# Performer layer: key maximum by a transposition on PE, norms behind the exponents, bfc ahead of Wo; experts: gate inside the first W1 product

## The chip, the cores and the metric

One core of a Trainium2 chip runs the whole kernel in one launch. The metric is the device time in microseconds; three runs of the kernel before gave 673.88, 672.17 and 673.33, median 673.33.

## The reference, cut to what matters

Three residual layers act on x (256 rows of 256 numbers): a cross attention over 4096 context rows, a Performer attention, and a mixture of experts. The last two matter here, each behind a layer norm.

```python
# Performer: 16 heads of 16 numbers, proj 44 x 16
td   = einsum('bhnd,md->bhnm', t * dn, proj)           # the exponents
diag = 0.5 * dn**2 * sum(t * t, axis=-1)               # the squared norms
mx   = max(td, -1) if is_query else max(td, (-1, -2))  # keys: one maximum per head over all rows
feat = ratio * (exp(td - diag - mx) + 1e-4)
k_sum = sum(kp, -2); d_inv = 1 / einsum('bhnm,bhm->bhn', qp, k_sum)
out  = einsum('bhmd,bhnm,bhn->bhnd', einsum('bhnm,bhnd->bhmd', kp, v), qp, d_inv)
y    = relu((out @ Wo.T + bo) @ Wfc.T + bfc)
# experts: 8 and a shared one, all computed for all 256 rows, F = 1024
probs = softmax(x @ Wg); the two largest are normalised to the weights cw
out   = sum_e cw[e] * (silu(x @ W1[e] + b1[e]) @ W2[e] + b2[e]) + 0.1 * shared(x)
```

## The kernel before, in words

Each engine has its own instruction queue, and the order in it is written out by hand; queues meet only through counting semaphores. PE is TensorE, DVE VectorE, ACT ScalarE, POOL GpSimd, SP issues transfers. `attention`, `performer` and `experts` each are one block, and all engines meet between blocks. Products that need precision split each operand into a rounded high part and a low part (what the rounding left) and sum three products (`part_products`, L165 to L170). `keep_busy` (L173 to L177), called `busy` in the Performer, is a dummy product on PE whose result nobody reads; each call is two instructions in the trace, as every matmul in float32 is.

**Performer** (L980 to L1304). Everything lives in one PSUM tile `ps` of eight banks; keys use banks 0 to 3, queries 4 to 7, each for two row tiles j times two halves of the heads. PE transposes the normalised rows, computes keys and queries transposed (L1075), and then, per tile and half, the exponents (L1085) and into the eight columns beside them the norms (L1087). DVE takes maxima of the key tiles (L1251), joins them (L1253) and takes the maxima of the query tiles (L1257). The key maximum over the 128 rows is an all-reduce over partitions on POOL (L1064). PE goes on with the values (L1111). DVE adds norm and maximum (`less`, L1260 and L1272) and subtracts it from the exponents (`shift`, L1244), first queries, then, behind the values' bias (L1267), keys; ACT takes the exponentials (L1196). PE transposes the query features (L1122), adds the constant feature's part with two products over `v_one` (L1130) and the key features' products (L1135). From that come denominators (L1145) and numerators (L1152); DVE inverts and multiplies per half (L1291, L1294), PE multiplies by Wo (L1160), ACT adds bo (`h_t`, L1206), PE puts bfc into banks 0 and 1 (L1167) and adds the products with Wfc (L1172), and DVE adds the rectified result to `x_res` (L1302). Between these steps PE has `busy` calls. On the side DVE makes the low part of the second expert's W1 (L1298).

**Experts** (L1307 to L1629). After the norm PE transposes z (L1412). DVE copies it to `zt` (L1577, L1580) for the gate, ACT makes the high part `zp` (L1520, L1522), DVE the low part (L1583). PE computes the gate (L1419), then W1 of experts 0 and 1 (`up`, L169), then W2 of 0 (`down`, L1447), and from there `up` of the next and `down` of the last in turns. `h_ps` has four banks of two tiles. DVE takes the gate's logits through some twenty small operations, each waiting for the one before, to `share` (L1587 to L1607), and only behind these makes W2's low part (`lo2`, L1547) and splits the activations in two halves (`split_act`: a cast L1556, a subtraction L1558 each). ACT makes the gate's exponentials, the silus (L1510), then the high parts of W2 of the next expert (L1500) and of W1 of the one behind that (L1494), which releases POOL's low part of that W1 (L1393).

## Time and profile before

| | us |
|---|---|
| median of three runs | 673.33 |
| profiled execution, its own time | 672.22 |
| its span, first to last instruction | 670.5 |
| PE busy | 651.6 (97%) |
| DVE busy | 511.7 (76%) |
| ACT busy | 414.2 (62%) |
| POOL busy | 271.8 (41%) |

The cross attention ends at about 522.7 us of the span, the Performer at 557.4, the experts at the end. All times in the rows below are microseconds from the start of the span. In a timeline a row is a run of like instructions: start, duration of the whole, engine, line, operation, output and inputs with their shapes, count, and in brackets how long the engine had been idle and for whom. PEld is the loading of weights into PE, which overlaps with its products.

### The profile page before, as it was taken

The numbers are of one execution on the slowest core, as the hardware profiler recorded it, in microseconds if no ns is written. First come the engines' busy times: TensorE is split into PE (matmuls) and PEld (weight loads), VectorE is DVE, ScalarE is ACT, GpSimd is POOL, SyncE is SP. The second block draws the span as 40 slices with busy tenths as digits, with TensorE's granted clock in tenths as the row PEclk, the third lists the DMA queues.
The fourth block names the chain that finished last, engine by engine and source line by source line (L and its number), as shares of the span: only waits on it lengthen the run. The fifth ranks groups of instructions, "written<-read, shape, count | busy, mean of one in ns | idle before, by whom it ended". The sixth has DMA issues, their size and how long they took to land. (4 is left out here: it accounts for less than half of the span.)

```text
span 670.5 us, 14507 instructions
## 1 busy us (share of the span) xinstructions
PE 651.6 (97%) x5192; PEld 522.4 (78%) x5192; DVE 511.7 (76%) x1008; ACT 414.2 (62%) x880; POOL 271.8 (41%) x211
## 2 busy tenths in 40 slices
PE   8899999999999999999999999999999999899998
PEld 7677777777777777777777777777775778899998
DVE  4888898877878777778767867877777685987674
ACT  5788788866566666665667566556563433655651
POOL 3544545533443443433443434434431300364640
PEclk9999999999999999999999999999999999999999
DMA  7111340010000010000000000000000301566500
GB/s 213 56 44 33 112 162 1 17 33 1 1 17 1 2 49 1 1 1 1 17 1 1 2 0 2 1 17 2 1 1 1 127 1 65 189 212 218 163 33 17
DMA packets 26164, 30.51 MB, mean 46 GB/s; under 512 B 4201, under 2 KB 23794, under 8 KB 26098
## 3 DMA queue, kind: packets, MB, share of 16 engines
q1 hardware_dynamic: 24594, 28.86, 13.1%
q8 instruction: 39, 0.64, 0.4%
q10 hardware_dynamic: 1504, 0.79, 0.4%
q14 instruction: 27, 0.22, 0.1%
HBM read 29.38 MB, written 0.26 MB: 44 GB/s over the span
## 5 line engine op out<-in xcount | busy, mean ns | idle before, releaser
L897 POOL TENSOR_TENSOR k_rms<-k_ss,neg_half 128x4 f32<-128x4 f32 x136 | 189.2, 1391 | 242.7 <-DVE k_ss L771 242.7
L603 ACT ACTIVATE probs<-s_ps,minus_bound 128x512 f32<-128x512 f32 x272 | 164.7, 689 | 97.0 <-PE s_ps L436 97.0
L169 PE MATMUL kv_ps<-w_quad,xn 128*128 128x512 f32 x816 | 206.9, 402 | 5.2 <-DVE xn L718 3.9
L765 DVE SCALAR_TENSOR_TENSOR probs_sum<-probs,tile_mask,probs_sum 128x512 f32<-128x512 f32 x264 | 191.8, 744 | 4.9 <-ACT probs L603 4.8
L169 PEld LDWEIGHTS kv_ps<-w_quad,xn 128*128 128x128 f32 x816 | 147.8, 188 | 44.5 <-DVE xn L718 6.6
L449 PE MATMUL o_ps<-probs,v 128*64 128x256 f32 x1088 | 132.6, 385 | 0.8 <-ACT probs L603 0.7
L436 PEld LDWEIGHTS s_ps<-q_parts,kt 64*128 64x128 f32 x1632 | 101.2, 185 | 26.6 <-issue 20.0
L436 PE MATMUL s_ps<-q_parts,kt 64*128 64x256 f32 x1632 | 115.0, 287 | 0.3 <-DVE kt L775 0.2
L449 PEld LDWEIGHTS o_ps<-probs,v 128*64 128x64 f32 x1088 | 71.9, 136 | 42.0 <-issue 10.9
L749 DVE SCALAR_TENSOR_TENSOR kn<-k_rms,kv_ps 128x256 f32<-128x256 f32 x136 | 56.8, 417 | 53.0 <-POOL k_rms L897 51.8
L771 DVE TENSOR_REDUCE k_ss<-k_sq 128x4 f32<-128x256 f32 x136 | 56.4, 415 | 21.0 <-ACT k_sq L581 20.0
L595 ACT ACTIVATE kt<-s_ps 128x256 fp32r<-128x256 f32 x136 | 44.8, 380 | 42.1 <-PE s_ps L420 42.1
L588 ACT ACTIVATE v<-kv_ps,tile_mask 128x256 f32<-128x256 f32 x136 | 66.9, 492 | 0.0
L775 DVE TENSOR_TENSOR kt<-s_ps,kt 128x256 fp32r<-128x256 f32 x136 | 51.4, 419 | 17.6 <-ACT kt L595 17.3
L581 ACT ACTIVATE k_sq<-kv_ps 128x256 f32<-128x256 f32 x136 | 53.9, 396 | 1.3 <-PE kv_ps L169 1.3
L420 PE MATMUL s_ps<-ident,kn 128*128 128x128 f32 x272 | 41.2, 273 | 0.7 <-DVE kn L749 0.5
L420 PEld LDWEIGHTS s_ps<-ident,kn 128*128 128x128 f32 x272 | 33.7, 140 | 10.0 <-DVE kn L749 0.9
L1393 POOL TENSOR_TENSOR w_first<-w_raw,w_first 128x2048 fp32r<-128x2048 f32 x4 | 21.8, 5462 | 29.2 <-ACT w_first L1494 29.2
L1556 DVE CAST e_act_p<-e_act_f 128x1024 fp32r<-128x1024 f32 x18 | 17.9, 994 | 20.4 <-PE e_y_ps L1447 20.3
L1510 ACT ACTIVATE e_act_f<-e_h_ps,e_b_now 128x256 f32<-128x256 f32 x72 | 27.9, 481 | 7.1 <-DVE e_act_p L1558 4.6
L169 PE MATMUL e_h_ps<-e_zp,w_first 128*128 128x256 f32 x240 | 28.6, 278 | 0.0
L169 PEld LDWEIGHTS e_h_ps<-e_zp,w_first 128*128 128x128 f32 x240 | 28.0, 188 | 0.3 <-issue 0.3
(212 smaller groups left out, 647.3 us busy)
## 6 DMA issues: line engine op xcount, KB each, us to landing
w_raw<-in_ffn_W SPq DMA_DIRECT2D x18, 1024.0 KB, 5.6
rows<-in_ctx SPq DMA_DIRECT2D x7, 512.0 KB, 4.0
w_raw<-in_L_xattn_Wkv SPq DMA_DIRECT2D x6, 256.0 KB, 3.4
wout<-in_L_xattn_Wout SPq DMA_DIRECT2D x4, 256.0 KB, 2.8
wq_raw<-in_L_xattn_Wq SPq DMA_DIRECT2D x3, 256.0 KB, 2.8
rows<-in_ctx SPq DMA_DIRECT2D x2, 256.0 KB, 5.3
w_raw<-in_L_xattn_Wkv ACTq DMA_DIRECT2D x2, 256.0 KB, 5.2
wq_raw<-in_L_xattn_Wq ACTq DMA_DIRECT2D x1, 256.0 KB, 4.3
```

What stands on the lines that cost most here:

```text
L169: last = nc.tensor.matmul(out, stationary(k, s), moving(k, m), start=n == 0, stop=n == len(terms) - 1)
L420: last = nc.tensor.transpose(kt_ps(n)[:, j * P:(j + 1) * P], kn[n % 2][:, j].rearrange("p c d -> p (c d)"), ident[:])
L436: last = nc.tensor.matmul(s_ps[b][c][:, j, :], kt[b][half, s, j * P:(j + 1) * P], q_parts[g % 2][half, j, m, :], start=term == 0, stop=ter ...
L449: last = nc.tensor.matmul(o_ps[g % 2][c * DH:(c + 1) * DH, j, :], v[n % V_RING][:, j, c, :], probs[n % P_RING][:, j, c, :], start=t == 0 a ...
L581: nc.scalar.activation(k_sq[n % 2][:].rearrange("p j c d -> p (j c d)"), kv_ps[n % 2][:, 0, :], ACT.Square, scale=DH ** -0.5).then_inc(sq_ ...
L588: nc.scalar.activation(v[n % V_RING][:].rearrange("p j c d -> p (j c d)"), kv_ps[n % 2][:, 1, :], ACT.Copy, scale=tile_mask[:, t:t + 1]).t ...
L603: nc.scalar.activation(probs[n % P_RING][:, :, c, :], s_ps[n % 2][c][:], ACT.Exp, bias=minus_bound[:]).then_inc(exp_done, 1)
L749: nc.vector.scalar_tensor_tensor(kn[n % 2][:], k_rms[n % 2][:].unsqueeze(3).to_broadcast([P, 2, 2, DH]), 1.0 / RMS_FLOOR, kv_ps[n % 2][:, ...
L765: nc.vector.scalar_tensor_tensor(total, probs[n % P_RING][:, :, c, :], seen, total, ALU.mult, ALU.add).then_inc(sum_done, 1)
L771: nc.vector.reduce_sum(k_ss[n % 2][:], k_sq[n % 2][:], AX_X).then_inc(ss_done, 1)
L775: nc.vector.tensor_tensor(kt[n % 2][:, 1, :], kt_ps(n), kt[n % 2][:, 0, :].bitcast(F32), ALU.subtract).then_inc(kt_lo, 1)
L897: nc.gpsimd.tensor_tensor(k_rms[n % 2][:].rearrange("p i c -> p (i c)"), k_ss[n % 2][:].rearrange("p i c -> p (i c)"), neg_half[:, 0:4], A ...
```

## The change

In the Performer the norm products leave the exponent groups. All exponents come first; the key maximum, now taken on each row, is transposed by PE (`top_turned`), reduced by DVE to one number per head, set on a 16x16 diagonal, and spread over all rows by a product with ones (`top_spread`). This product and the norms of queries and keys come behind the last exponents, into free columns of banks 0 to 3. POOL's all-reduce is gone. DVE makes the `less` of queries and keys directly after each other; the values on PE wait for it. The keys' first shift stands before the values' bias, the second behind it and behind a new sum `v_sum` of the two value tiles, with which the constant feature needs one product. The bfc products go in front of Wo, in banks 0 and 7, in place of dummies; other dummies are dropped.

In the experts the high part of `zp` is made as each half is transposed, the low part from PSUM, and the copies `zt` for the gate behind these. `up` of expert 0 starts without the gate; the gate's products come in it behind its first bank.

```diff
-        top_key = sb("top_key", [P, 2, H])
+        top_key, top_all, top_diag = sb("top_key", [P, H]), sb("top_all", [H, 1]), sb("top_diag", [H, H])
+        top_spread, v_sum = sb("top_spread", [P, H]), sb("v_sum", [P, H * VW])
...
-        def diagonal(n):
-            b = bank(n, 0, 0)
-            return ps[:, b:b + 4, EW:EW + HH]
+
+        def norm_ps(n):
+            at = 488 if n == QUERY else EW
+            return ps[:, 0:4, at:at + HH]
+
+        top_turned_ps, top_spread_ps = ps[0:H, 0, 360:360 + P], ps[:, 0, 496:496 + H]
+
+        def fc_ps(j):
+            return ps[:, 7 if j else 0, 0:D]
...
                                     ALU.subtract).then_inc(ew.w1_lo, 1)
-            pool.wait_ge(key_top, 1)
-            nc.gpsimd.partition_all_reduce(top_key[:, 1, :], top_key[:, 0, :], P, bass.bass_isa.ReduceOp.max).then_inc(key_top_all, 1)
             nc.gpsimd.iota(ew.number[:], [[1, E]], base=0, channel_multiplier=0).then_inc(ew.numbered, 1)
...
-            def exponents_of(n, parts_done, done):
+            def exponents_of(n, j, parts_done, done):
+                for half in range(KD):
+                    if j == 0:
+                        pe.wait_ge(parts_done, half + 1)
+                    last = part_products(nc, ps[:, bank(n, j, half), 0:EW], lambda k, s: qk_t[:, n, half, s, j * P:(j + 1) * P],
+                                         lambda k, s: proj_p[:, s, :], 1)
+                last.then_inc(done, 1)
+
+            def norms_of(n):
                 for j in range(QT):
                     for half in range(KD):
-                        if j == 0:
-                            pe.wait_ge(parts_done, half + 1)
-                        b = ps[:, bank(n, j, half)]
-                        part_products(nc, b[:, 0:EW], lambda k, s: qk_t[:, n, half, s, j * P:(j + 1) * P],
-                                      lambda k, s: proj_p[:, s, :], 1)
-                        last = nc.tensor.matmul(b[:, EW:EW + HH], qk_sq[:, n, half, j * P:(j + 1) * P],
-                                                diag_bd[:], start=True, stop=True)
-                    last.then_inc(done, 1)
+                        last = nc.tensor.matmul(norm_ps(n)[:, 2 * j + half, :], qk_sq[:, n, half, j * P:(j + 1) * P], diag_bd[:],
+                                                start=True, stop=True, skip_group_check=True)
+                return last
...
             pe.wait_ge(fw.blocks_done, 2)
-            exponents_of(KEY, k_lo, k_exponents)
-            pe.wait_ge(q_lo, KD)
-            exponents_of(QUERY, q_lo, q_exponents)
+            for j in range(QT):
+                exponents_of(KEY, j, k_lo, k_exponents)
+            exponents_of(QUERY, 0, q_lo, q_exponents)
             pe.wait_ge(key_top, 1)
+            nc.tensor.transpose(top_turned_ps, top_key[:], ident[:]).then_inc(top_turned, 1)
+            exponents_of(QUERY, 1, q_lo, q_exponents)
+            pe.wait_ge(top_placed, 1)
+            norms_of(QUERY)
+            norms_of(KEY)
+            nc.tensor.matmul(top_spread_ps, ones[0:H, :], top_diag[:], start=True, stop=True, skip_group_check=True).then_inc(diagonals_done, 1)
...
             pe.wait_ge(k_shifted, 2)
             pe.wait_ge(v_kept, 1)
-            for j in range(QT):
-                nc.tensor.matmul(ps[0:PAIR, 0, 0:NPAIR * 2 * VW], feat_eps[:], v_one[:, j].rearrange("p h d -> p (h d)"),
-                                 start=j == 0, stop=False, skip_group_check=True)
+            nc.tensor.matmul(ps[0:PAIR, 0, 0:NPAIR * 2 * VW], feat_eps[:], v_sum[:], start=True, stop=False, skip_group_check=True)
...
                 last.then_inc(o_done, 1)
-            busy(7, 3)
+            for j in range(QT):
+                nc.tensor.matmul(fc_ps(j), ones[0:1, :], spread["bfc"][0:1, :], start=True, stop=False)
...
                 if k == 0:
-                    busy(7, 3)
-            for j in range(QT):
-                nc.tensor.matmul(ps[:, j, 0:D], ones[0:1, :], spread["bfc"][0:1, :], start=True, stop=False)
-            busy(7, 1)
+                    busy(3, 2)
             for k in range(KD):
                 pe.wait_ge(ht_kept, k + 1)
                 for j in range(QT):
-                    last = nc.tensor.matmul(ps[:, j, 0:D], h_t[:, k, j * P:(j + 1) * P], w["Wfc"][:, k, :],
+                    last = nc.tensor.matmul(fc_ps(j), h_t[:, k, j * P:(j + 1) * P], w["Wfc"][:, k, :],
...
-            busy(7, 3)
+            busy(3, 1)
...
-            nc.vector.tensor_tensor(top_key[:, 0, :], top[:, KEY, 0:KD].rearrange("p k h -> p (k h)"),
+            nc.vector.tensor_tensor(top_key[:], top[:, KEY, 0:KD].rearrange("p k h -> p (k h)"),
...
-            for j in range(QT):
-                dve.wait_ge(q_exponents, j + 1)
-                last = nc.vector.reduce_max(top[:, QUERY, 2 * j:2 * j + 2], exponents(QUERY, j), AX_X)
-            last.then_inc(own, 1)
+            dve.wait_ge(q_exponents, 1)
+            nc.vector.reduce_max(top[:, QUERY, 0:2], exponents(QUERY, 0), AX_X)
+
+            dve.wait_ge(top_turned, 1)
+            nc.vector.reduce_max(top_all[:], top_turned_ps, AX_X).then_inc(top_found, 1)
+            dve.wait_ge(top_found, 1)
+            nc.vector.tensor_scalar(top_diag[:], ident[0:H, 0:H], top_all[:], None, ALU.mult).then_inc(top_placed, 1)
+            dve.wait_ge(q_exponents, 2)
+            nc.vector.reduce_max(top[:, QUERY, 2:4], exponents(QUERY, 1), AX_X).then_inc(own, 1)
             dve.wait_ge(own, 3)
-            nc.vector.tensor_tensor(less[:, QUERY], diagonal(QUERY), top[:, QUERY], ALU.add).then_inc(q_less, 1)
+            dve.wait_ge(diagonals_done, 1)
+            nc.vector.tensor_copy(top_spread[:], top_spread_ps).then_inc(spread_kept, 1)
+            nc.vector.tensor_tensor(less[:, QUERY], norm_ps(QUERY), top[:, QUERY], ALU.add).then_inc(q_less, 1)
+            dve.wait_ge(spread_kept, 1)
+            nc.vector.tensor_tensor(less[:, KEY].rearrange("p (j k) h -> p j (k h)", j=QT).rearrange("p j (k h) -> p j k h", k=KD),
+                                    norm_ps(KEY).rearrange("p (j k) h -> p j k h", j=QT),
+                                    top_spread[:].rearrange("p (k h) -> p k h", k=KD).unsqueeze(1).to_broadcast([P, QT, KD, HH]),
+                                    ALU.add).then_inc(k_less, 1)
             dve.wait_ge(q_less, 1)
             for j in range(QT):
                 shift(QUERY, j, q_shifted)
+            dve.wait_ge(k_less, 1)
             dve.wait_ge(v_done, 1)
+            shift(KEY, 0, k_shifted)
...
-            last.then_inc(v_kept, 1)
-            dve.wait_ge(key_top_all, 1)
-            nc.vector.tensor_tensor(less[:, KEY].rearrange("p (j k) h -> p j (k h)", j=QT).rearrange("p j (k h) -> p j k h", k=KD),
-                                    diagonal(KEY).rearrange("p (j k) h -> p j k h", j=QT),
-                                    top_key[:, 1, :].rearrange("p (k h) -> p k h", k=KD).unsqueeze(1).to_broadcast([P, QT, KD, HH]),
-                                    ALU.add).then_inc(k_less, 1)
-            dve.wait_ge(k_less, 1)
-            for j in range(QT):
-                shift(KEY, j, k_shifted)
+            last.then_inc(v_biased, 1)
+            dve.wait_ge(v_biased, 1)
+            nc.vector.tensor_tensor(v_sum[:], v_one[:, 0].rearrange("p h d -> p (h d)"), v_one[:, 1].rearrange("p h d -> p (h d)"),
+                                    ALU.add).then_inc(v_kept, 1)
+            shift(KEY, 1, k_shifted)
...
-                last = nc.vector.scalar_tensor_tensor(x_res[:, j, :], ps[:, j, 0:D], 0.0, x_res[:, j, :], ALU.max, ALU.add)
+                last = nc.vector.scalar_tensor_tensor(x_res[:, j, :], fc_ps(j), 0.0, x_res[:, j, :], ALU.max, ALU.add)
...
-            keep_busy(nc, h_ps[:, 0, :], ident[:], x_res[:, 0, :], 2)
-            pe.wait_ge(zt_kept, KD)
-            pe.wait_ge(wg_in, 16)
-            for j in range(QT):
-                for k in range(KD):
-                    last = nc.tensor.matmul(gate_ps[:, j * E:(j + 1) * E], zt[:, k, j * P:(j + 1) * P], wg[:, k, :],
-                                            start=k == 0, stop=k == KD - 1)
-            last.then_inc(logits_done, 1)
-            pe.wait_ge(zp_done, 1)
-
-            def up(t):
+            pe.wait_ge(zp_done, KD)
+
+            def gates():
+                pe.wait_ge(zt_kept, KD)
+                pe.wait_ge(wg_in, 16)
+                for j in range(QT):
+                    for k in range(KD):
+                        last = nc.tensor.matmul(gate_ps[:, j * E:(j + 1) * E], zt[:, k, j * P:(j + 1) * P], wg[:, k, :],
+                                                start=k == 0, stop=k == KD - 1)
+                last.then_inc(logits_done, 1)
+
...
                     last.then_inc(up_done, 1)
+                    if gated and b == 0:
+                        gates()
...
-            up(Turn(0, 2))
+            up(Turn(0, 2), gated=True)
...
-            act.wait_ge(zt_done, KD)
-            nc.scalar.activation(zp[:, 1, 0, :], y_ps[1][:, 0, :], ACT.Copy).then_inc(zp_hi, 1)
-            act.wait_ge(zt_kept, 1)
-            nc.scalar.activation(zp[:, 0, 0, :], y_ps[0][:, 0, :], ACT.Copy).then_inc(zp_hi, 1)
+            for k in range(KD):
+                act.wait_ge(zt_done, k + 1)
+                nc.scalar.activation(zp[:, k, 0, :], y_ps[k][:, 0, :], ACT.Copy).then_inc(zp_hi, 1)
...
-            dve.wait_ge(zt_done, 1)
-            nc.vector.tensor_copy(zt[:, 0, :], y_ps[0][:, 0, :]).then_inc(zt_kept, 1)
-            dve.wait_ge(zt_done, KD)
-            dve.wait_ge(zp_hi, 1)
-            nc.vector.tensor_copy(zt[:, 1, :], y_ps[1][:, 0, :]).then_inc(zt_kept, 1)
-            dve.wait_ge(zp_hi, KD)
-            dve.wait_ge(zt_kept, KD)
-            nc.vector.tensor_tensor(zp[:, :, 1, :], zt[:], zp[:, :, 0, :].bitcast(F32), ALU.subtract).then_inc(zp_done, 1)
+            for k in range(KD):
+                dve.wait_ge(zp_hi, k + 1)
+                nc.vector.tensor_tensor(zp[:, k, 1, :], y_ps[k][:, 0, :], zp[:, k, 0, :].bitcast(F32), ALU.subtract).then_inc(zp_done, 1)
+            for k in range(KD):
+                nc.vector.tensor_copy(zt[:, k, :], y_ps[k][:, 0, :]).then_inc(zt_kept, 1)
```

## Rows read from the trace of the kernel before

**Rows 1.** The page: busy time of the engines, and the chain that ended last.

```profile
PE 651.6 (97%) x5192; PEld 522.4 (78%) x5192; DVE 511.7 (76%) x1008; ACT 414.2 (62%) x880; POOL 271.8 (41%) x211
...
PE e_y_ps L1447 6%; PE e_h_ps L169 6%; DVE e_act_p L1558 1%; PE e_h_ps L177 0%; PE e_y_ps L1462 0%; PE e_bias_ps L1462 0%; DVE w_first L1547 0%; DVE e_act_p L1556 0%; DVE e_picked L1605 0%; PE e_gate_ps L1419 0%; PE e_bias_ps L1482 0%; ACT 
```

**Rows 2.** Windows: span, busy us (instructions) of PE, PEld, DVE, ACT, POOL; clock, DMA.

```profile
536.40:541.90 5.50, 4.92 (x39) 4.27 (x37) 5.20 (x10) 2.32 (x3) 0.39 (x1) 1.00 0.00 0
...
574.80:583.90 9.10, 7.21 (x55) 6.46 (x53) 9.07 (x5) 2.90 (x7) 5.01 (x2) 1.00 0.52 189
...
583.90:668.00 84.10, 83.92 (x721) 83.72 (x720) 60.77 (x57) 44.36 (x69) 38.07 (x12) 1.00 0.41 137
```

**Rows 3.** Timeline of the Performer's key maximum: start, us, engine, line, operation.

```profile
532.36 0.89 DVE L1251 TENSOR_REDUCE f_top<-f_ps 128x16 f32<-128x704 f32 x1
...
534.70 0.17 DVE L1253 TENSOR_TENSOR f_top_key<-f_top 128x16 f32<-128x16 f32 x1
...
536.39 1.87 PEld L1111 LDWEIGHTS f_ps<-f_Wv,f_zt 128*128 128x128 f32 x16
...
537.75 1.69 DVE L1244 TENSOR_TENSOR f_feats<-f_ps,f_less 128x704 f32<-128x704 f32 x2
...
538.00 0.39 POOL L1064 PARTITION_ALL_REDUCE f_top_key<-f_top_key  x1 [5.59 <-issue]
...
539.35 0.75 DVE L1267 TENSOR_TENSOR f_v_one<-f_ps,f_bv 128x256 f32<-128x256 f32 x2
```

**Rows 4.** Timeline, PE's weight loads of eps and context products.

```profile
541.98 0.69 PEld L1130 LDWEIGHTS f_ps<-f_v_one,f_feat_eps 128*88 128x88 f32 x4 [0.66 <-DVE f_feats L1244]
...
542.74 2.74 PEld L1135 LDWEIGHTS f_ps<-f_v_one,f_feats 128*88 128x88 f32 x32
```

**Rows 5.** Timeline, from the second Wo group to the next block.

```profile
551.47 0.84 PEld L1160 LDWEIGHTS f_ps<-f_o_t,f_Wo 128*128 128x128 f32 x4
...
552.31 0.91 ACT L1206 ACTIVATE f_h_t<-f_ps,f_bo 128x256 f32<-128x256 f32 x2 [7.77 <-PE f_ps L1160]
...
552.64 0.72 PEld L1167 LDWEIGHTS f_ps<-f_bfc,ones 1*128 1x128 f32 x4 [0.33 <-issue]
...
554.01 1.70 PEld L1172 LDWEIGHTS f_ps<-f_Wfc,f_h_t 128*128 128x128 f32 x8
...
555.73 0.86 DVE L1302 SCALAR_TENSOR_TENSOR x_res<-f_ps,x_res 128x256 f32<-128x256 f32 x2 [2.23 <-PE f_ps L1172]
...
555.96 1.46 PE L177 MATMUL f_ps<-f_Wq,ident 128*128 128x256 f32 x6
...
557.71 0.75 DVE L965 BATCH_NORM_STATS2 e_stats<-x_res 128x6 f32<-128x256 f32 x2 [1.13 <-PEq L987]
```

**Rows 6.** Timeline of the experts' start: high part, gate, first W1 product, share.

```profile
561.45 0.38 ACT L1520 ACTIVATE e_zp<-e_y_ps 128x256 fp32r<-128x256 f32 x1 [8.23 <-PE e_y_ps L1412]
...
562.41 0.97 PEld L1419 LDWEIGHTS e_gate_ps<-e_wg,e_zt 128*128 128x128 f32 x8 [0.54 <-DVE e_zt L1580]
...
563.29 5.72 PEld L169 LDWEIGHTS e_h_ps<-e_zp,w_first 128*128 128x128 f32 x48
...
563.50 0.39 DVE L1587 MAX8 e_logit_top<-e_gate_ps 128x8 f32<-128x8 f32 x2 [0.35 <-PE e_gate_ps L1419]
...
565.06 1.28 ACT L1510 ACT_TABLE_LOAD   x1 [0.33 <-PE e_h_ps L169]
...
569.48 2.29 DVE L1547 TENSOR_TENSOR w_first<-w_raw,w_first 128x2048 fp32r<-128x2048 f32 x1
```

**Rows 7.** Timelines of POOL, DVE and PE where the first expert is split.

```profile
573.80 4.88 POOL L1393 TENSOR_TENSOR w_first<-w_raw,w_first 128x2048 fp32r<-128x2048 f32 x1 [13.73 <-ACT w_first L1494]
...
574.27 5.50 DVE L1558 TENSOR_TENSOR e_act_p<-e_act_f,e_act_p 128x1024 fp32r<-128x1024 f32 x1
...
579.82 3.10 PE L1447 MATMUL e_y_ps<-w_first,e_act_p 128*128 128x256 f32 x24 [1.89 <-DVE e_act_p L1558]
...
603.79 1.74 DVE L1556 CAST e_act_p<-e_act_f 128x1024 fp32r<-128x1024 f32 x1 [3.27 <-PE e_y_ps L1447]
```

More of the change, by code:

```diff
@@ L1017, in performer @@
         k_exponents, q_exponents = sem("f_k_exponents"), sem("f_q_exponents")
-        key_tops, key_top, key_top_all = sem("f_key_tops"), sem("f_key_top"), sem("f_key_top_all")
+        key_tops, key_top, top_turned = sem("f_key_tops"), sem("f_key_top"), sem("f_top_turned")
+        top_found, top_placed, diagonals_done = sem("f_top_found"), sem("f_top_placed"), sem("f_diagonals_done")
+        v_biased, spread_kept = sem("f_v_biased"), sem("f_spread_kept")
         k_less, q_less, k_shifted, q_shifted = sem("f_k_less"), sem("f_q_less"), sem("f_k_shifted"), sem("f_q_shifted")
```

2 lines of the change are left out of this document (added).

## The prediction

> **What bounds the kernel now.** I read the busy shares of the page first, then the chain that ended last, then the windows by stage, and only then the timeline of each engine. PE is busy for 97% of the span, and the part of the chain that the page shows starts at 557.7 us and is nearly all PE work of the experts [rows 1]. From 583.9 us PE does not idle until the end [rows 2]: whatever is won or lost before that point moves the end by the same amount, and nothing behind it is changed. Ahead of it are two places where PE does not set the pace. In the Performer, PE is filled with dummy products (L177), so its busy share hides the real chain, which runs PE, DVE and ACT in turn; I follow it from the first exponents (530.6) to the residual add (L1302). In the first two experts PE idles 1.9 us in the stretch from 574.8 to 583.9 [rows 2]. The reader is to see there that the second half of L1558 takes 5.50 us, where the other halves take 1.23, and lies just behind the start of the POOL subtraction L1393 [rows 7].
>
> Sums are made on the profiled execution: span 670.5, its own time 672.22, so 1.72 lies around the span. The median shown, 673.33, is 1.11 above it. I add the sum to the median.
>
> **Performer, key maximum and norms.** Until 530.6 nothing changes. Before, each of the eight exponent groups on PE ended with a norm product; now the groups follow without them, and DVE's first maximum still starts at 532.36, since the low part of the queries (L1240) leaves DVE only then. One maximum over 704 columns takes 0.89 and back to back they come every 0.80 to 0.85 [rows 3], so the second ends at 534.04 and the key top is there at 534.25, where it stood at 534.87 (534.70 + 0.17) [rows 3]: 0.6 earlier. Then a new chain: the transposition on PE (no row of this shape; a matmul that begins alone took 0.28 to 0.29 to its end, and 0.06 to be released) ends at 534.62, while DVE is in its maximum of the first query tile (534.20 to 535.09). The maximum over 16x128 and the small product behind it are new shapes. From below two 0.17 instructions bound them, by the 128x16 row of [rows 3], from above two of 0.89. I take 0.29 and 0.24, by the 128-column and the 128x8 operations elsewhere in the trace, as they are nearest in size. PE gets its release at 535.63, just as its second query group has been issued.
>
> Now eight norm products and the spread product, two weight loads each, 18 in all. The loads of L1111 come every 0.117 (16 in 1.87) [rows 3], those of the gate every 0.12 (8 in 0.97) [rows 6]; a product that sits between others costs at most its full load, 0.19. Bounds 1.9 to 3.4, I take 2.05 by the nearest rows, and 0.2 for the last one's drain: 537.88. DVE copies the spread and makes both sums (0.37 to 0.6, by the 0.17 to 0.19 of such small operations): the first query shift starts at 538.25, where it was 537.75 [rows 3], 0.5 later. The value products L1111, which used to lie under the query maxima, now wait for the key sums: 538.35 plus 2.05 is 540.4, before 538.45. DVE ends the query shifts at 539.94 and idles 0.46, since the first key shift is queued behind the wait for the values. Then 0.89 (key shift 0), 0.66 for the two value adds as they pipeline (0.75 with the end of the second [rows 3]), 0.44 for the new 128x272 sum (bounds 0.29 for 128 columns, 0.69 for 512), 0.89 (key shift 1): 543.29, before 541.92 (540.23 + 1.69 for two such shifts). That is +1.37. The PE transposes of the queries, behind the later values, end at 543.05 and stay just covered. The eps product is one call in place of two: of the 0.76 between the first load of L1130 and that of L1135 [rows 4] half goes, -0.37. The exponentials of the keys are there in time (544.1 for the second tile, PE needs it at 545.1). Term: **+1.0**, bounds 0.0 (the shift chain no later than PE's own work) to +2.9 (all new shapes at their upper ends).
>
> What goes for this is the all-reduce on POOL [rows 3]. DVE did not wait for it: behind L1267 (539.35 + 0.75) it goes on at 540.02 without idling. Its removal by itself is worth nothing; it was hidden behind the query side.
>
> **Performer, bfc and Wo.** Up to L1160 everything follows the DVE reciprocals, so the bfc products in place of three dummies stay covered (0.72 of loads against 1.16; cover gone would cost at most 0.7). The second Wo group waited for its dummies (551.47 against its input at 551.29): -0.12. Then the real gain: ACT has h_t ready at 552.31 + 0.47 = 552.78 and the other half at 553.22, but PE first loads bfc (552.64) and a dummy and starts Wfc only at 554.01 [rows 5]. With these gone Wfc starts 0.06 behind h_t, at 552.72 after the 0.12: **-1.29**, and its second k finds its input (553.1) before it needs it (553.6). What is late next is L1298 on DVE, which ends at 553.49, earlier than the Wfc result (554.44), so it does not bind.
>
> **Performer, end.** The residual add ends at 555.73 + 0.86 = 556.59, but the six dummy instructions on PE end at 555.96 + 1.46 = 557.42, and DVE starts the next block at 557.71 [rows 5]. At the change of block before this one DVE was last (522.68) and started 0.32 later (523.00). With two dummy instructions PE ends 0.9 sooner and DVE binds: 555.30 + 0.32 = 555.62 against 557.71 is -2.09 with the last term in it, so **-0.80** of its own (bounds 0 and -0.83). Start of the experts: +1.0 - 1.29 - 0.80 = about -1.1.
>
> **Experts, on PE.** Times here are in the old frame. The high parts on ACT follow each transposed half: 561.23 to 561.61, then 561.51 to 561.89 (0.38 each, 0.28 apart); the low parts on DVE (0.42 each) end at 562.46, and W1 starts at 562.52, where the gate products started at 562.41 [rows 6]. The gate cost the same 0.88 before its successor could load, in front of W1 or inside it. So PE ends both W1 products 0.1 later than before and gains nothing: the two copies that DVE now makes later had not been the limit, as the gate only went first.
>
> **Experts, on DVE and ACT.** The gate now comes behind twelve products (12 x 0.118 = 1.42, from 48 loads in 5.66 [rows 6]): the logits come at 565.03 instead of 563.50, 1.53 later. The small operations from the logits to the share, 6.06 us, have to run ahead of L1547, which starts then at 571.0 [rows 6]; the first half of L1556 follows at 573.21 and that of L1558 at 573.93 to 575.16. On ACT the table load no longer waits for W1 (565.06 was the end of the first bank [rows 6]); it comes behind the exponentials at 566.25, the eight silus (3.02 to 3.08) end at 570.6, two 1.92 copies follow 1.8 apart, and POOL is released at 574.27 instead of 573.80. PE needs the first half of the split at 574.95; it comes at 575.2, 0.2 late.
>
> The price lies in the second half. [Rows 7] show POOL released at 573.80, in the middle of a DVE cast (to 574.23), POOL ending at 578.68, and the L1558 that followed the cast held until then: POOL had waited for one DVE operation and then had its way for 4.45 us before the next. The cast of 603.79 is held in the same way (1.74 for 0.69). So I let POOL, released at 574.27, wait for the end of the first half of L1558 (575.16) and hold its successors to 579.61. Then the cast needs 0.55 more and L1558 1.25: PE gets the second half at 581.5, before 579.82. **+1.69**, and its idle time there grows from 1.9 to some 3. Everything behind it shifts as it is, PE bound.
>
> The Trainium skill ("SBUF — State Buffer", section "SBUF: two separate sides") says that DVE and GpSimd share a port pair as an exclusive lock for a whole instruction, DVE casts in a fast mode and operations with two SBUF inputs included, the loser fully blocked. The rows agree, and by that rule the term stays +1.69; it says nothing of who goes next when DVE's queue is full, on which rival 1 hangs.
>
> **Sum.** +1.0 - 1.29 - 0.80 + 1.69 = +0.6: 672.22 + 0.6 = 672.8 for an execution like the profiled one, 673.33 + 0.6 = **673.9** for the median. No difference that can be told: a measurement of this kernel tells about 0.3%, 2 us, from nothing.
>
> **Rivals.**
> 1. POOL never gets between. If the operations in DVE's queue keep POOL out until the second L1558 has begun (575.9), PE has its input at 577.1 and does not idle: -1.1 - 1.9 = -3.0, 670.3. For it: POOL comes later relative to PE. Against: it would have to be 1.6 later than I work out, and at 573.80 it won against a full DVE queue. 0.14.
> 2. POOL comes in 0.37 or more sooner relative to DVE, inside the first cast (to 573.90). Then both halves of L1558 lie behind it: the first half at 579.4, the second at 581.3, while PE does both after 579.5 and ends at 585.6 instead of 582.9: +2.7 - 1.1 = +1.6, 674.9. For it: the margin is small. Against: ACT's chain is made of measured pieces. 0.15.
> 3. The granted clock falls. It is 1.00 in every stage, also where PE idles 0.6 and is busy 4.92 of 5.5 [rows 2]. Now PE has two us of eight-column products, a pause of half a us and sparser value products in a row (535.6 to 540.4), and fewer dummies later. At 1.2 GHz in place of 2.4 that stretch's 4.9 us of work could take up to that much more; as half of it is loads and waits I take +3 on top of the sum: +3.6, 677. The point from which it decides is the norm products. No row shows the lower level, and PE's idling of 1.9 us at 577.9 did not bring it. 0.12. The Trainium skill ("TensorE: Matmul & The Clock Gate", "Part 1: The HAM clock gate") has the clock set by how busy PE was of late, between just these two levels; by it the thinned stages are what could bring the fall, no run yet shows it.
> 4. The gain at the end of the Performer does not come, because the change of block takes its time from something else than PE's dummies: +0.6 + 0.8 = +1.4, 674.7. 0.07.
>
> **How the numbers follow.** The forecast has the remaining 0.52, with its own range 672.6 to 675.2 (the terms' likely errors, 0.7, and the spread of medians). Faster than 671.3 is nearly only rival 1: 0.15. Slower than 675.3 is rival 3, and the upper part of rival 2, rival 4 and of the first term's bounds: 0.24. Range 670.7 to 676.4: it leaves out half of rival 1 and most of rival 3.
>
> **What would show it.** Right: the first query shift 0.3 to 0.8 later, L1244's last of the keys about 1.4 later and context about 1.0; Wfc directly behind h_t; experts starting 0.8 to 1.4 earlier; the logits 1.5 later against the block's start; the second L1556 or L1558 of the first expert held behind POOL and PE idle some 3 us there. Wrong: a clock below 1.00; the second L1558 at 1.23 us; an exponent or norm stage more than 1 us off.

## The result

| | before | changed |
|---|---|---|
| median of six runs each, same chip | 672.08 us | 676.13 us |
| ratio, 95% interval | | 1.0049 [1.0037, 1.0060] |
| profiled execution, its own time (span) | 672.22 (670.5) | 675.89 (674.2) |
| mean granted clock of the profiled execution | 1.000 | 0.992 |

The change costs 4 us where I had forecast +0.6. The time itself lies in the range (to 676.4), near rival 3, the fall of the clock, which I had given 0.12. That it lies in the range is partly luck: I had counted from 673.33, the median of three runs, and the median of six is 672.08. Counted from there the same range ends at 675.2, below the measured time.

First the windows of the changed kernel, with the columns of [rows 2] (the fraction before the last two figures is the granted clock):

```profile
536.00:538.00 2.00, 1.47 (x13) 1.35 (x12) 0.55 (x5) 0.00 (x0) 0.00 (x0) 1.00 0.00 0
...
538.00:540.00 2.00, 1.97 (x12) 1.97 (x13) 1.57 (x2) 1.18 (x2) 0.00 (x0) 0.72 0.00 0
...
540.00:542.00 2.00, 2.00 (x9) 1.82 (x8) 0.82 (x2) 0.40 (x1) 0.00 (x0) 0.50 0.00 0
...
542.00:544.00 2.00, 2.00 (x17) 1.81 (x17) 1.97 (x5) 0.79 (x1) 0.00 (x0) 0.92 0.00 0
...
574.00:580.00 6.00, 3.80 (x31) 3.31 (x29) 5.97 (x3) 1.57 (x4) 5.71 (x2) 0.99 0.95 346
...
580.00:590.00 10.00, 9.03 (x48) 8.41 (x49) 8.63 (x11) 5.01 (x6) 0.00 (x0) 0.67 0.55 189
...
590.00:674.00 84.00, 81.49 (x702) 81.29 (x700) 54.03 (x52) 41.77 (x68) 38.17 (x12) 1.00 0.35 119
```

Two stretches stand out: from 538.9 to 542.3 and from 579.9 to 586.7 the clock is at 1.2 GHz instead of 2.4 (0.50 of full speed where a window lies inside). Before, the clock was 1.00 in every window [rows 2]. Ahead of the first, PE works on the norms (536 to 538: busy 1.47 of 2) and pauses; ahead of the second it idles 2.2 us in the window from 574 to 580 and one more after it.

The timeline of DVE and of PE's weight loads, which answers to [rows 3]. The whole block starts 0.32 us earlier than before, which belongs to the attention; I count it out below.

```profile
532.01 1.68 DVE L1264 TENSOR_REDUCE f_top<-f_ps 128x16 f32<-128x704 f32 x2
...
537.90 1.68 DVE L1257 TENSOR_TENSOR f_feats<-f_ps,f_less 128x704 f32<-128x704 f32 x2
...
541.18 0.89 DVE L1257 TENSOR_TENSOR f_feats<-f_ps,f_less 128x704 f32<-128x704 f32 x1 [1.60 <-PE f_ps L1128]
...
543.12 0.88 DVE L1257 TENSOR_TENSOR f_feats<-f_ps,f_less 128x704 f32<-128x704 f32 x1
```

```profile
535.20 1.86 PEld L1097 LDWEIGHTS f_ps<-f_diag_bd,f_qk_sq 128*128 128x128 f32 x16 [0.29 <-DVE f_top_diag L1274]
...
538.03 2.74 PEld L1128 LDWEIGHTS f_ps<-f_Wv,f_zt 128*128 128x128 f32 x16 [0.66 <-DVE f_less L1282]
```

Both maxima of the keys come in one run (1.68 for two), and the first query shift is at 537.90, that is 538.22 with the 0.32 added back, forecast 538.25. The values L1128 then take 2.74 us of loads instead of 1.87 (the clock falls 0.8 us behind their start), and DVE idles 1.60 in front of the first key shift instead of the 0.46 I had worked out. The last one starts at 543.12, which is 543.44 in the same way where I had 542.40: the 1.0 us between is this longer wait.

The end of the Performer, which answers to [rows 5]; first PE's loads, then DVE:

```profile
554.30 1.59 PEld L1185 LDWEIGHTS f_ps<-f_Wfc,f_h_t 128*128 128x128 f32 x8 [0.53 <-ACT f_h_t L1219]
```

```profile
555.90 0.86 DVE L1325 SCALAR_TENSOR_TENSOR x_res<-f_ps,x_res 128x256 f32<-128x256 f32 x2 [0.72 <-PE f_ps L1185]
...
557.30 0.75 DVE L965 BATCH_NORM_STATS2 e_stats<-x_res 128x6 f32<-128x256 f32 x2 [0.54 <-PEq L987]
```

Wfc now starts 0.53 after PE's last load of Wo, released by ACT, and DVE's next block starts 0.54 after its last instruction (I had taken 0.32, from the change of block that comes earlier in the kernel). The experts begin at 557.30 instead of 557.71: with the 0.32 counted out the Performer as a whole gained 0.09 us, not 1.1. The missing 1.0 is the longer wait at the low clock.

The experts, which answer to [rows 6, 7]: PE's loads, then DVE, POOL and PE.

```profile
562.04 1.48 PEld L169 LDWEIGHTS e_h_ps<-e_zp,w_first 128*128 128x128 f32 x12 [1.28 <-DVE e_zp L1603]
...
563.45 0.97 PEld L1444 LDWEIGHTS e_gate_ps<-e_wg,e_zt 128*128 128x128 f32 x8
```

```profile
564.55 0.38 DVE L1609 MAX8 e_logit_top<-e_gate_ps 128x8 f32<-128x8 f32 x2 [1.90 <-PE e_gate_ps L1444]
...
570.53 2.29 DVE L1572 TENSOR_TENSOR w_first<-w_raw,w_first 128x2048 fp32r<-128x2048 f32 x1
...
573.45 1.23 DVE L1583 TENSOR_TENSOR e_act_p<-e_act_f,e_act_p 128x1024 fp32r<-128x1024 f32 x1
...
574.60 5.07 DVE L1581 CAST e_act_p<-e_act_f 128x1024 fp32r<-128x1024 f32 x1
```

```profile
573.81 5.30 POOL L1416 TENSOR_TENSOR w_first<-w_raw,w_first 128x2048 fp32r<-128x2048 f32 x1 [14.22 <-ACT w_first L1520]
```

```profile
580.98 5.49 PE L1473 MATMUL e_y_ps<-w_first,e_act_p 128*128 128x256 f32 x24 [3.08 <-DVE e_act_p L1583]
...
587.57 5.92 PE L169 MATMUL e_h_ps<-e_zp,w_first 128*128 128x256 f32 x48
```

Against the start of the block W1 starts at 4.74 (before, the gate at 4.70), the logits are 1.46 later, POOL is released 0.42 later. The last three fences show what I call the hold, DVE blocked while POOL works: POOL's L1416, released at 573.81 inside the first subtraction (573.45 to 574.68), ends at 579.11, and the second cast L1581, which needs 0.69, takes 5.07. PE idles 3.08 us, starts the second half 1.57 later than before in the block's own time, and then needs 5.49 for what took 3.10, at the low clock.

So the +3.67 us of the profiled span are made of: attention -0.32, Performer -0.09, the hold +1.57, and +2.51 between 581 and 588, where the first product of the next expert (583.90 before [rows 2], 587.57 now) stands 3.67 later. From there on nothing changes.

### The profile page after: what moved, and what is told of

Same layout as the page of the kernel before. It is cut to its first block and busy times, and to the rows that moved or that the text cites. A ratio compares the mean times of both kernels' runs of the same rounds, so it can differ in the third digit from the quotient of the medians.

```text
span 674.2 us, 14471 instructions
## 1 busy us (share of the span) xinstructions
PE 652.7 (97%) x5175; PEld 523.0 (78%) x5175; DVE 508.8 (75%) x1013; ACT 413.4 (61%) x880; POOL 271.0 (40%) x210
## 5 line engine op out<-in xcount | busy, mean ns | idle before, releaser
L1581 DVE CAST e_act_p<-e_act_f 128x1024 fp32r<-128x1024 f32 x18 | 22.5, 1251 | 26.4 <-PE e_y_ps L1473 26.4
L1416 POOL TENSOR_TENSOR w_first<-w_raw,w_first 128x2048 fp32r<-128x2048 f32 x4 | 22.3, 5566 | 29.7 <-ACT w_first L1520 29.7
```

## The experiments

Each kernel ran beside the kernel before on the same chip; there are three groups, each on a chip of its own, and each begins with its own "before" (the row "changed" is the result above, whose before stands there). The records of each run give its mean granted clock over the whole kernel. The values come in steps: 1.000, where the clock never fell, then 0.997, 0.995 and so on, the lower the longer it stayed down. That is why I list times by clock, too: the median us, and in brackets the number of runs.

```
kernel                       clock 1.000  0.997       0.995       0.992      0.990      ratio [95%]
before, first group          671.94 (12)  673.70 (11)
changed                                               675.17 (1)  676.13 (4) 677.39 (1) 1.0049 [1.0037, 1.0060]
Performer alone              671.00 (4)   672.46 (2)  673.83 (3)  674.94 (3)            1.0000 [0.9984, 1.0015]
experts alone                673.78 (1)   675.50 (3)  676.41 (2)                        1.0042 [1.0026, 1.0059]
changed, POOL waits                                   674.34 (2)  675.91 (3) 676.14 (1) 1.0041 [1.0025, 1.0057]
changed, PE filled                        673.77 (8)  674.68 (3)                        1.0019 [1.0009, 1.0029]
before, second group         672.41 (8)   673.75 (8)
bfc part alone               670.05 (3)   671.49 (5)                                    0.9972 [0.9961, 0.9983]
changed, early low part      668.40 (1)   669.97 (3)  671.29 (4)                        0.9963 [0.9949, 0.9978]
before, early low part       669.86 (5)                                                 0.9953 [0.9941, 0.9966]
  and the bfc part           668.04 (4), one more at 0.999: 668.54                      0.9928 [0.9915, 0.9941]
before, third group          671.98 (9)   673.54 (13), one at 0.999: 672.24
norms part + early low part  670.96 (4)   672.29 (4)  673.58 (3)  674.12 (1)            0.9991 [0.9978, 1.0003]
  with four dummies          671.94 (10)              674.24 (2)                        0.9989 [0.9978, 1.0000]
bfc, early, changed experts  667.77 (5), one more at 0.999: 668.15                      0.9923 [0.9909, 0.9937]
```

The run times of one kernel at one clock still differ by up to 1.1 us, and the chips by some 0.4. The profiled executions tell the stages apart more finely. The next table has the length of the Performer (from the start of its first layer norm on DVE to that of the experts'), the first part of the experts (from there to PE's third W1 product, 583.90 before), and where the clock was low.

| profile | Performer | experts' first part | low clock, us of the span |
|---|---|---|---|
| before | 34.71 | 26.19 | none |
| changed | 34.62 | 30.27 | 538.9 to 542.3, 579.9 to 586.7 |
| Performer alone | 35.86 | 27.73 | 537.0 to 543.8, 581.3 to 584.8 |
| experts alone | 34.71 | 29.27 | 582.6 to 586.1 |
| changed, POOL waits | 34.62 | 26.88 | 538.8 to 542.3, 583.2 to 590.1 |
| changed, PE filled | 35.91 | 27.79 | 537.1 to 544.1 |
| bfc part alone | 32.62 | 26.19 | none |
| changed, early low part | 34.62 | 24.10 | 539.1 to 542.6 |
| before, early low part | 34.72 | 24.04 | none |
| and the bfc part | 32.63 | 24.05 | none |
| norms part + early low part | 38.01 | 24.06 | 537.2 to 544.2 |
| with four dummies | 36.67 | 24.05 | none |
| bfc, early, changed experts | 32.62 | 24.10 | only behind PE's last product |

My theory after the result: the terms of the sum were right, and the rest are two falls of the clock, one from the sparse norm stage, one from PE's idling while POOL holds DVE. Rival: the second follows from the first, or the terms themselves are off.

**1. The Performer alone.** The function `performer` of the changed kernel, all else of before.

> The changed Performer with the experts of before. My theory: the clock falls for some 3.4 us at the norms and values, which eats the gain of about 1.1 us, so the experts start 0.1 us earlier than before (0.3 us more or less from the attention's side); the experts then run as before: the second L1558 held some 5.5 us, PE idle 1.9 us, clock 1.00 there. Total -0.1 us against before, no difference. Rival (the second fall of the clock follows from the first, or from the Performer's fewer dummies, not from PE's longer idling in the experts): the clock falls again behind 578 us and the total is +2.4 us.

Windows of the profiled execution (674.63 us, clock 0.992):

```profile
538.00:540.00 2.00, 1.75 (x8) 1.75 (x9) 1.79 (x4) 0.96 (x2) 0.00 (x0) 0.50 0.00 0
...
578.00:582.00 4.00, 2.11 (x16) 1.91 (x15) 4.00 (x3) 1.31 (x4) 2.64 (x2) 0.92 0.44 179
...
582.00:586.00 4.00, 4.00 (x21) 3.74 (x20) 3.56 (x4) 0.88 (x2) 0.00 (x0) 0.65 0.37 97
```

Where the clock stayed at 1.000 the gain is 671.94 - 671.00 = 0.94 us, close to the 1.1 of the sum, and at lower clocks it is gone. The medians (673.20 and 672.60) show no clear difference, as expected. But I had expected 1.00 in the experts, and the window at 582 shows 0.65, behind 1.9 us of idling (2.11 busy of 4). The runs of before fit: 11 of 23 have 0.997. Idling of 1.9 us does bring the clock down, in some executions.

Where the first fall begins says something about its cause. PE's products there, and one window:

```profile
537.09 0.60 PE L1123 MATMUL f_ps<-f_top_diag,ones 16*128 16x16 f32 x2
...
538.25 3.78 PE L1128 MATMUL f_ps<-f_Wv,f_zt 128*128 128x128 f32 x16 [0.56 <-DVE f_less L1282]
```

```profile
537.00:538.00 1.00, 0.69 (x4) 0.56 (x3) 0.20 (x2) 0.00 (x0) 0.00 (x0) 0.51 0.00 0
```

The clock is low from 537.0 on, at the end of the norm products, and the pause of 0.56 us before the values only comes at 537.7. In the profiles of kernels 4 and 9 it also fell ahead of this pause; in those of the changed kernel and of kernels 3 and 6 it fell 0.8 to 1.3 us behind the start of the values. The pause cannot be what the first three needed.

**2. The experts alone.** The function `experts` of the changed kernel, all else of before.

> The Performer of before with the changed experts. My theory: clock 1.00 through the Performer; the logits come 1.5 us later in the block, POOL's low part gets in ahead of the second cast (5.1 us instead of 0.7), PE idles 3.1 us, and this alone brings the clock down for some 6.8 us, worth 2.5 us: +1.6 + 2.5 = +4.1 us. Rival (the fall needs the thin Performer too): clock 1.00 throughout, +1.6 us.

```profile
536.00:538.00 2.00, 2.00 (x18) 2.00 (x18) 1.41 (x4) 0.00 (x0) 0.00 (x0) 1.00 0.00 0
...
540.00:542.00 2.00, 1.78 (x17) 1.53 (x14) 1.97 (x4) 1.11 (x2) 0.00 (x0) 1.00 0.00 0
...
578.00:582.00 4.00, 0.92 (x8) 0.72 (x7) 3.97 (x4) 0.37 (x1) 2.32 (x2) 1.00 0.63 251
...
582.00:586.00 4.00, 4.00 (x23) 3.95 (x22) 3.88 (x3) 1.21 (x4) 0.00 (x0) 0.58 0.15 31
```

No fall in the Performer (536, 540: 1.00), and one behind the idling (578: busy 0.92 of 4; 582: 0.58). The rival that the second needs the first is out. The late gate and the hold come to +1.84 in the one run at 1.000, forecast +1.69. For the whole +4.1 was expected, and +3.1 is the difference of the medians: in this profile the clock was low for 3.4 us and not for 6.8, and the fall cost 1.5 us (29.27 less 26.19 and 1.57) and not 2.5.

**3. POOL waits for the split.** In the changed kernel:

```diff
+            pool.wait_ge(act_lo, 2)
             run(pool, lo1, 2, E1, 2)
```

> The changed kernel, but POOL's first low part of W1 in the experts waits until DVE has split both halves of expert 0. My theory (order on the pair of ports): the second cast takes 0.7 us and the second subtraction 1.2, PE starts the second half of W2 at once after the first and does not idle there, so the clock stays at 1.00 behind 570 us: 1.2 to 1.6 us of the split and 1.5 of the old wait and 2.5 us of the clock come back, -5 to -5.6 us against the changed kernel, about -1.3 us against before. Rival (the price is DVE's lateness itself, or W1's low part is then late for its product): the idle time only moves, less than 1.5 us comes back.

```profile
574.51 0.69 DVE L1582 CAST e_act_p<-e_act_f 128x1024 fp32r<-128x1024 f32 x1
...
575.23 1.23 DVE L1584 TENSOR_TENSOR e_act_p<-e_act_f,e_act_p 128x1024 fp32r<-128x1024 f32 x1
...
576.71 2.27 DVE L1573 TENSOR_TENSOR e_w_second<-w_raw,e_w_second 128x2048 fp32r<-128x2048 f32 x1
...
578.91 0.68 DVE L1582 CAST e_act_p<-e_act_f 128x1024 fp32r<-128x1024 f32 x1
...
579.62 5.46 DVE L1584 TENSOR_TENSOR e_act_p<-e_act_f,e_act_p 128x1024 fp32r<-128x1024 f32 x1
```

```profile
576.71 7.29 POOL L1416 TENSOR_TENSOR w_first<-w_raw,w_first 128x2048 fp32r<-128x2048 f32 x1 [17.15 <-DVE e_act_p L1584]
```

```profile
584.14 8.56 PE L169 MATMUL e_h_ps<-e_zp,w_first 128*128 128x256 f32 x48 [2.43 <-POOL w_first L1416]
```

The cast takes 0.69 and the subtraction 1.23, as expected. But POOL, released at 576.71, meets DVE's L1573 that starts at the same time, and takes 7.29 us. It lets two operations of DVE by, L1573 and the cast behind it (to 579.59), then needs 4.41 us of its own, during which the next subtraction is held (5.46 instead of 1.23). Its part of W1 is late, PE idles 2.43 in front of the next expert and runs at the low clock there (8.56 for 5.9 us of work). 675.5 us instead of some 670.8: my expectation failed and the rival held. (The Trainium skill, "SBUF — State Buffer", section "SBUF: two separate sides", has whichever of the two starts first hold the shared ports for its whole instruction while the other is blocked. The trace agrees: the held subtraction, which needs 1.23, ends 1.08 behind POOL, at 585.08.) A wait only moved the collision; what has to go is work of DVE's at that place.

**4. PE filled.** In the changed kernel, six dummy products before the wait for the second half of expert 0:

```diff
-            def down(t):
+            def down(t, fill=0):
...
                 for half in range(2):
+                    if half == 1:
+                        keep_busy(nc, gate_ps[:, 0:NQ], ident[:], zt[:, 0, :], fill)
                     pe.wait_ge(act_lo, t.n * 2 + (1 + half))
...
-            down(Turn(0, 2))
+            down(Turn(0, 2), 6)
```

> The changed kernel with six dummy products (twelve instructions, 2.8 us) on PE in front of the wait for the second half of the split of expert 0. The cast is held by POOL as before. My theory: PE starts the second half at the same time (about 581.0), but the clock stays at 1.00 there, and only the 2.5 us of the second slow stretch come back. Rival (the clock's fall is not from idling at this place): nothing comes back, or the dummies cost up to 0.5 us.

```profile
578.00:582.00 4.00, 3.77 (x22) 3.10 (x21) 3.97 (x2) 0.00 (x0) 3.00 (x2) 1.00 0.86 329
...
582.00:586.00 4.00, 3.74 (x27) 3.55 (x28) 3.96 (x5) 2.10 (x5) 0.00 (x0) 1.00 0.05 12
```

```profile
582.26 3.11 PE L1475 MATMUL e_y_ps<-w_first,e_act_p 128*128 128x256 f32 x24 [0.50 <-DVE e_act_p L1585]
...
586.36 5.92 PE L169 MATMUL e_h_ps<-e_zp,w_first 128*128 128x256 f32 x48
```

The clock is 1.00 there, and the hold is untouched: the second half starts 23.69 into the block, as in the changed kernel (23.68), and takes 3.11 instead of 5.49. The experts' first part is 27.79 against 30.27, so this low stretch was worth 2.5 us, as expected, and came from PE's idling. The medians show less of it, some 2 us (1.0019 of before against 1.0049), and the profiled execution pays 1.3 us more than the changed kernel's in the Performer, where its clock was low for longer. All 11 runs have 0.997 or less; in the profiled one the only low stretch is the Performer's.

**5. The bfc part alone.** The kernel before with the bfc products ahead of Wo, in banks 0 and 7, and the dummies as in the change.

> The kernel before with only bfc ahead of Wo and the fewer dummies behind it; key maximum, norms and experts as before. My theory: Wfc starts 1.3 us earlier and the next block another 0.8 us, -2.1 us where the clock stays at 1.00 (669.8 against 671.9 for such runs of before), and a clock that falls as often as before, as the norm stage is as dense as before. Rival (the fewer dummies of this part are what thins the Performer): the mean clock is below 0.997 in most runs, and the gain is gone in the median.

```profile
551.66 0.91 ACT L1207 ACTIVATE f_h_t<-f_ps,f_bo 128x256 f32<-128x256 f32 x2 [7.54 <-PE f_ps L1164]
...
552.18 1.59 PEld L1173 LDWEIGHTS f_ps<-f_Wfc,f_h_t 128*128 128x128 f32 x8 [0.54 <-ACT f_h_t L1207]
...
553.78 0.86 DVE L1303 SCALAR_TENSOR_TENSOR x_res<-f_ps,x_res 128x256 f32<-128x256 f32 x2 [0.72 <-PE f_ps L1173]
...
555.18 0.75 DVE L965 BATCH_NORM_STATS2 e_stats<-x_res 128x6 f32<-128x256 f32 x2 [0.54 <-PEq L987]
```

Wfc starts 0.52 behind the start of ACT's first h_t, and DVE is in the next block 1.40 after the start of its residual add, where it was 1.98 [rows 5]. The Performer is 32.62 long instead of 34.71, -2.09, as forecast; the run times at equal clock give -2.36 (672.41 to 670.05). Three of eight runs are at 1.000 and none is below 0.997, as with the kernel before in this group (8 of 16), so these dummies are not what thinned the Performer.

**6 and 7. The low part of W2 ahead of the logits.** DVE idles 1.9 us for the logits in the changed kernel and has 2.3 us of work behind the share that needs nothing of it:

```diff
+            lo2(Turn(0, 2))
             dve.wait_ge(logits_done, 1)
...
             last.then_inc(share_done, 1)
-            lo2(Turn(0, 2))
             split_act(Turn(0, 2))
```

In the changed kernel:

> The changed kernel, with DVE's low part of expert 0's W2 (2.3 us) made while DVE waits for the gate's logits (1.9 us idle there) instead of behind the share. My theory: the share comes 0.4 us later, both halves of the split of expert 0 are done (574.7) before POOL's subtraction can hold one of them, PE does not idle between the halves, no low clock behind 575 us; the fall at the norms stays. -1.7 - 1.9 - 2.5 = -6 us against the changed kernel, 670 to 671. Rival (as in the run in which POOL waited: the hold only moves to the next operations, and PE idles there): less than 2 us.

```profile
562.39 2.28 DVE L1572 TENSOR_TENSOR w_first<-w_raw,w_first 128x2048 fp32r<-128x2048 f32 x1
...
572.42 0.69 DVE L1581 CAST e_act_p<-e_act_f 128x1024 fp32r<-128x1024 f32 x1
...
573.14 1.23 DVE L1583 TENSOR_TENSOR e_act_p<-e_act_f,e_act_p 128x1024 fp32r<-128x1024 f32 x1
...
574.93 6.05 DVE L1572 TENSOR_TENSOR e_w_second<-w_raw,e_w_second 128x2048 fp32r<-128x2048 f32 x1
```

```profile
573.85 4.99 POOL L1416 TENSOR_TENSOR w_first<-w_raw,w_first 128x2048 fp32r<-128x2048 f32 x1 [14.43 <-ACT w_first L1520]
```

```profile
574.31 5.93 PE L1473 MATMUL e_y_ps<-w_first,e_act_p 128*128 128x256 f32 x48
```

DVE fills its wait (562.39 to 564.67) and is through with the split at 574.37; POOL, released at 573.85, waits for DVE's last subtraction and then holds L1572 (6.05 instead of 2.3), for which nobody waits. PE runs all 48 products of W2 in one (5.93). 670.6 us, as expected (670 to 671).

In the kernel before:

> The kernel before with the same move. The logits are there 1.5 us earlier than in the changed one, so DVE is 1.9 us late for them, but the 2.3 us behind the share are gone. My theory: no operation of the first split is held, PE's 1.9 us of idling go and with them the falls of the clock that half of the runs of before have: 670.0 at clock 1.00, and nearly all runs there, so -2.3 us in the median. Rival (the later share holds PE up, or POOL comes in all the same): 0 to +1 us.

669.86 us, and all five runs at 1.000, where the kernel before has 8 of 16. At equal clock that is -2.55 us (672.41 in this group), by the profiles -2.15 (24.04 for 26.19). Expected 670.0.

**8. Both.** The edits of 5 and 7 on the kernel before.

> Both together on the kernel before: bfc ahead with fewer dummies, and the early low part; key maximum, norms and gate as before. If the two are independent: -2.1 - 1.9 = 667.9 at clock 1.00 and most runs there. Rival (fewer dummies bring the clock down): 669 to 671.

668.11 us, 0.9928 of before. The two add up: by the profiles -2.08 in the Performer and -2.14 in the experts. (The run times at 1.000 give -1.8 on top of kernel 7 where they gave -2.36 for the bfc part alone, which shows how far five runs can be trusted.)

**9 and 10. The norms part alone, and filled.** Key maximum, norms and values of the change, without the bfc part and with the early low part; then with two dummy products of 128 columns behind each group of norms:

```diff
             norms_of(QUERY)
+            keep_busy(nc, ps[:, 1, 360:360 + P], ident[:], w["Wq"][:, 0, 0:P], 2)
             norms_of(KEY)
+            keep_busy(nc, ps[:, 1, 360:360 + P], ident[:], w["Wq"][:, 0, 0:P], 2)
```

> Only the key maximum by transposition with the norms and values behind the exponents, on the kernel before with the early low part (669.9 us, never a slow stretch in five runs). bfc and all dummies as before. My theory: the sparse norm products and the pause before the values are what brings the Performer's clock down: +1.0 us at clock 1.00 (670.9), and most runs below 1.00 with the slow stretch between 536 and 544 us, 672.0 to 673.5 in the median. Rival (the fewer dummies of the bfc part are needed for the fall): clock 1.00, 670.9.

> The same with four dummy products of 128 columns (eight instructions, 0.94 us) among the norm products, on the path. My theory: +0.9 us by the dummies, but the clock stays at 1.00 in more of the runs: 671.8 at clock 1.00. Rival (the clock answers to the pauses, not to the columns that PE works on): as many slow runs as without, and 0.9 us later.

Windows of the first, then of the second:

```profile
536.00:540.00 4.00, 3.44 (x22) 3.31 (x22) 2.21 (x6) 0.97 (x2) 0.00 (x0) 0.66 0.00 0
...
540.00:544.00 4.00, 4.00 (x17) 3.47 (x17) 1.83 (x4) 1.40 (x2) 0.00 (x0) 0.50 0.00 0
```

```profile
536.00:540.00 4.00, 3.44 (x29) 3.22 (x29) 1.55 (x6) 0.08 (x1) 0.00 (x0) 1.00 0.00 0
...
540.00:544.00 4.00, 3.81 (x31) 3.38 (x29) 3.35 (x6) 2.29 (x3) 0.00 (x0) 1.00 0.00 0
```

Alone the part costs 670.96 - 669.86 = +1.1 us at clock 1.000 (two chips; each against its own before it is +1.5). The profiles are sharper: filled, the Performer is 36.67 at full clock, and from the first norm load to the values it takes 3.83 instead of the changed kernel's 2.83, so 1.00 is the dummies and 36.67 - 34.71 - 1.00 = +0.96 the part (forecast +1.0). 8 of the 12 runs without the four dummies are below 1.000 and up to 3.2 us longer; the profiled one has the low clock from 537.2 to 544.2, which costs it 2.3 us. All the dummies of before stand in this kernel, so the fewer dummies of the bfc part are not needed for the fall. Filled, 10 of 12 stay at 1.000, for 1.0 us of dummies, and the medians are the same (672.29, 672.04). PE waits 0.56 us before the values in both, so it pauses as long, and only the work ahead of the pause is denser. That and the falls ahead of the pause (kernel 1) speak against the rival, by which only the pauses count.

**11. The best version with the changed experts.** Kernel 8 with the changed start of the experts.

> The best version so far (bfc ahead, early low part, 668.1 us), with the changed start of the experts (low part from PSUM, gate inside the first W1 product). My theory: with the low part of W2 out of the way the late gate costs only its 0.1 us on PE: 668.2, clock 1.00. Rival (the change to the experts pays once nothing holds DVE): below 667.6; or the idle 1.1 us before W1 without dummies brings the clock down: 669 to 670.

667.85 us, 0.9923 of before, the lowest median, 0.3 us under kernel 8 at clock 1.000. But the changed start of the experts is no gain: its first part takes 24.10 us against 24.05, the Performer 32.62 against 32.63. The cost of some 0.1 that I expected held, and the rival that it pays is out in the profile.

## Why the prediction was right or wrong

- **Key maximum and norms, +1.0:** right. +0.96 by the profile at full clock. The first query shift was off by 0.03 us.
- **bfc, -1.29, and the end of the block, -0.80:** the sum of the two, -2.09, came to the digit, but by two misses that cancel. Alone (kernel 5), the residual add starts 1.51 earlier in the block, and from it to the next block it is 0.58 shorter, as the change of block took 0.54 and not 0.32.
- **Experts on PE, +0.1:** right (0.04).
- **Experts on DVE, +1.69:** right in place, cause and size: logits +1.46 (1.53), POOL's release +0.42 (0.47), the cast held, PE +1.57. The rule I used for who goes next, that POOL waits for the one DVE operation that is running and then holds what follows, fits every first hold at this place but one: in kernel 3 POOL let two operations by.
- **Sum, +0.6:** it is what the parts give at full clock (+0.96 - 2.09 + 1.57 = +0.4 by the profiles, -0.94 + 1.84 = +0.9 by the run times), and no run of the changed kernel was there.
- **The step that failed is the clock.** The sum has it at 1.00 throughout, and the falls stand only in rival 3, with 0.12. "A clock below 1.00" was my own sign of being wrong, and all six runs show it. The fall at the norms I had in the right place, but as unlikely, and at +3; 8 of 12 runs of the norms alone have it, and it costs 1.0 us in the changed kernel's profile (0.09 instead of 1.1 gained) and 2.3 in that of kernel 1, where the clock was low for twice as long. The fall in the experts I had nowhere: "PE's idling of 1.9 us at 577.9 did not bring it" was read from one execution, while half of the runs of before have 0.997 and take 1.6 to 1.8 us more. That argument should have stood the other way: my own term lengthened the idling to 3.1 us, which all but one of the experts' runs answered with a fall. Its price was 2.5 us.
- **Rival 1** (-3.0, POOL kept out) is what the early low part brought about by other means; it did not come by itself. **Rival 2** did not occur, and of **rival 4** only 0.2 us, the longer change of block.

That the runs of before below 1.000 have their low stretch behind 578 us was not seen in a profile of their own. The evidence is that the Performer alone, with the same experts, shows it there, and that such runs vanish with the idling: of the kernels 7, 8 and 11 no run is below 0.999, and in the one profiled at 0.999 the low clock comes behind PE's last product. Why one execution falls and the next doesn't is open.

## What to carry to other kernels

Where one profile shows PE idling for two microseconds at full clock, that says little on the next run: take the mean clock of many runs, and price each new or longer pause of PE with a stretch at the low clock behind it. DVE's casts and its subtractions of two operands in SBUF, and POOL's subtraction, exclude each other here; when POOL is released within such a train of DVE operations, it lets the running one by (once two), and then the rest of the train waits for it. A wait on POOL only moved the collision, and filling PE only kept the clock, but moving DVE's independent work (2.3 us here) into an earlier idle time of DVE gained 2.1 us, as much as the best part of the change.

## What the runs showed of the hardware

- Run times of one kernel on one core stand in steps that go with the mean granted clock: 671.94 and 673.70 for the kernel before, 671.0, 672.5, 673.8, 674.9 for the Performer alone. The two steps of before, 1.8 us apart, are most of its spread (671.8 to 674.0).
- In the six profiles whose clock fell in the Performer, PE had worked through sixteen instructions of eight columns (1.95 us). In three of them the clock fell at 537.0 to 537.3, ahead of PE's pause of 0.56 us, in three behind it. Four products of 128 columns among them (1.0 us) kept the clock in 10 of 12 runs, where 4 of 12 stayed without.
- In the experts the clock fell 1.9 us into a pause of 3.1 (changed), 1.5 us into one of 2.4 (POOL waits), 1.0 us behind one of 3.1 (experts alone) and 0.7 us behind one of 1.9 (Performer alone). A low stretch of 3.4 us cost 1.0 to 1.5 us, one of 6.8 us 2.3 to 2.5.
- POOL's subtraction over 128x2048 took 4.4 to 4.6 us of its own, and 7.29 from its release when two DVE operations (2.27 and 0.68 us) went first.
